# L0 cross-attention: the keys' reciprocal norms spread to their head's rows by transfers, and the scores at another place of the step

## What is computed

```python
def rmsnorm(x, gamma, eps=1e-08):
    n = jnp.linalg.norm(x, axis=-1, keepdims=True) * x.shape[-1] ** (-0.5)
    return x / jnp.maximum(n, eps) * gamma
xn = layernorm(x, ln_x_g, ln_x_b)
ln = layernorm(latents, ln_l_g, ln_l_b)
q = (ln @ Wq)...                      # 16 heads of 64
kv = jnp.concatenate([xn @ Wkv, ln @ Wkv], axis=1)
qn = rmsnorm(q, qn_g) * scale
kn = rmsnorm(k, kn_g)
sim = jnp.einsum('bhid,bhjd->bhij', qn, kn)
sim = jnp.where(padded_mask[:, None, None, :], sim, max_neg)
attn = jax.nn.softmax(sim.astype(jnp.float32), axis=-1).astype(sim.dtype)
out = jnp.einsum('bhij,bhjd->bhid', attn, v)
return out.transpose(0, 2, 1, 3).reshape(b, m, h * d) @ Wout + bout
```

## Time and profile before

| | |
|---|---|
| median of 3 runs | 3399.54 us (3392.83 to 3403.0) |
| the profiled execution | 3395.09 us, its span 3392.6 us |
| TensorE busy | 2876.9 us (85%) |
| VectorE, ScalarE, GpSimd busy | 1615.2, 1080.2, 508.4 us |
| granted TensorE clock, mean | 0.92 |
| DMA | 215.22 MB, 63 GB/s over the span |
| key steps of the L0 cross-attention | 91.0 to about 1310 us, 64 steps |

### The profile page before, as it was taken

How to read it: one execution, slowest core, us unless ns; L and a number is a source line. 1 busy time by engine, 2 the same in 40 slices (tenths; PEclk the granted TensorE clock), 3 DMA queues, 4 the chain that set the end, 5 groups by cost and what they waited for, 6 DMA issues and landing times. The chain is left out here.

```text
span 3392.6 us, 44228 instructions
## 1 busy us (share of the span) xinstructions
PE 2876.9 (85%) x17908; PEld 1943.1 (57%) x17908; DVE 1615.2 (48%) x3651; ACT 1080.2 (32%) x1931; POOL 508.4 (15%) x280
## 2 busy tenths in 40 slices
PE   4899999999999998579999968998964769588756
PEld 2465656666665665445565634665952449577644
DVE  4445454545545443425555545773531340355454
ACT  2233333333333331213555536641321423111121
POOL 2011020202011000000000002770010140244200
PEclk8899999999999999689999989998977879899877
DMA  3000000000000000030101000114857149423101
GB/s 132 0 1 22 1 22 22 1 22 1 22 1 22 1 1 4 27 134 21 40 20 40 1 6 23 45 35 176 312 192 252 55 149 311 166 87 108 31 1 31
DMA packets 80798, 215.22 MB, mean 63 GB/s; under 512 B 5328, under 2 KB 53992, under 8 KB 73944
## 3 DMA queue, kind: packets, MB, share of 16 engines
q1 hardware_dynamic: 77624, 204.32, 18.0%
q0 software_dynamic: 2976, 8.13, 0.7%
HBM read 201.33 MB, written 10.58 MB: 62 GB/s over the span
## 5 line engine op out<-in xcount | busy, mean ns | idle before, releaser
L1328 PE MATMUL L_xattn_bank<-L_xattn_keys_tok,L_xattn_probsT 119*128 119x257 f32 (+1 forms) x1792 | 437.6, 389 | 1.4 <-ACT L_xattn_probsT L1161 1.4
L1262 PE MATMUL L_xattn_wide<-L_xattn_keys_feat,weights_a 128*128 128x512 f32 (+2 forms) x1024 | 388.3, 524 | 3.0 <-DVE L_xattn_max L997 1.3
L1328 PEld LDWEIGHTS L_xattn_bank<-L_xattn_keys_tok,L_xattn_probsT 119*128 119x128 f32 (+1 forms) x1792 | 324.3, 189 | 112.3 <-ACT L_xattn_probsT L1161 42.6
L1155 ACT ACTIVATE L_xattn_scores<-L_xattn_scores,L_xattn_neg_max 128x833 f32<-128x833 f32 x128 | 119.7, 983 | 627.8 <-DVE L_xattn_neg_max L1002 627.8
L1262 PEld LDWEIGHTS L_xattn_wide<-L_xattn_keys_feat,weights_a 128*128 128x128 f32 x1024 | 190.6, 192 | 157.9 <-issue 128.8
L2267 DVE TENSOR_TENSOR_SCAN L_attn_state<-L_attn_decay,L_attn_banks 128x1024 f32<-128x1024 f32 x80 | 182.7, 2286 | 69.5 <-PE L_attn_banks L2469 61.5
L987 DVE TENSOR_TENSOR L_xattn_k_normed<-L_xattn_wide,L_xattn_k_normed 128x834 f32<-128x834 f32 x128 | 125.5, 1022 | 172.8 <-PE L_xattn_wide L1276 172.8
L1544 DVE CUSTOM_DVE_ANT_0 L_xattn_scores<-L_xattn_banks,L_xattn_mask 128x512 f32<-128x512 f32 (+1 forms) x256 | 131.5, 570 | 151.8 <-issue 151.8
L1082 POOL TENSOR_TENSOR L_xattn_keys_tok<-L_xattn_keys_tok,weights_a 119x1792 f32<-119x1792 f32 (+2 forms) x24 | 61.1, 2545 | 939.2 <-DVE L_xattn_keys_tok L922 939.2
L2373 POOL TENSOR_TENSOR L_attn_state<-L_attn_state,L_attn_C_rows 128x1024 f32<-128x1024 f32 x80 | 188.7, 2360 | 70.2 <-DVE L_attn_state L2267 70.1
L2469 PEld LDWEIGHTS L_attn_banks<-L_attn_B_diagonal,L_attn_dt_u_tok 128*128 128x128 f32 x1280 | 150.2, 193 | 66.3 <-issue 64.7
(11 more groups left out here) (498 smaller groups left out, 4691.2 us busy)
## 6 DMA issues: line engine op xcount, KB each, us to landing
L_xattn_ctx_feat<-in_ctx_feat SPq DMA_DIRECT2D x24, 1601.0 KB, 10.3
L_ffn_expert_w<-in_x_L_ffn SPq DMA_DIRECT2D x16, 2056.0 KB, 8.6
L_ffn_expert_w<-in_x_L_ffn SPq DMA_DIRECT2D x15, 1028.0 KB, 7.6
L_ffn_expert_w<-in_x_L_ffn SPq DMA_DIRECT2D x15, 1024.0 KB, 8.4
L_xattn_keys_tok<-in_ctx_tok SPq DMA_DIRECT2D x8, 1547.0 KB
L_attn_C_rows<-L_attn_c_rows SPq DMA_DIRECT2D x48, 256.0 KB, 3.3
L_xattn_ctx_tok<-in_ctx_tok SPq DMA_DIRECT2D x8, 1536.0 KB
L_xattn_ctx_tok_and_one<-in_ctx_tok SPq DMA_DIRECT2D x8, 1536.0 KB
```

What stands on the lines that cost most here:

```text
L1262: last = nc.tensor.matmul(wide[:, 2 * h + c, 0:n], wk[:, k, p * P:(p + 1) * P], xnT[b % 2][:, k, a:a + n], start=(k == 0), stop=(k == KT - 1))
L1328: last = nc.tensor.matmul(bS[:, 0:D + 1], pT[0:r, c, a, :, :].rearrange("p h q -> p (h q)"), xn[b % 2][0:r, t, :], start=(t == 0), stop=(t ...
```

## The change

The four products of `spread` go. In their place ScalarE, behind the second activation of `key_rnorm`, issues eight DMAs: for each quarter j and head h one, whose source is the single SBUF row `rk[32 j + h]` of 417 numbers and whose destination is the 64 rows of that head in a new SBUF tile `spread[:, j, :]`. `keys_normed` waits for all eight (8 x 16 on `k_scale_moved`), and multiplies two SBUF operands.

Since the four banks are then free once `key_clamp(s + 1)` has read bank 0, `scores(s)` waits for that clamp and for the keys of its own step, not for those of s + 1. `swap_max`, `shift` and `exponentials` of step s move into iteration s, behind the scores; `keys_normed(s + 1)` moves behind `shift(s)` on VectorE, ahead of the context work and of `divide`. TensorE's list becomes: keys half 0, turn_weights 0 and 1, keys half 1, turn_weights 2 and 3, turn_mixed, 4 tiles of mix, means, 2 tiles, scores, apply_v, 5 tiles, swap_max, 3 tiles. The tiles of mix are taken in another order, so that the first need ScalarE's copies alone.

```diff
@@ @@
+    MIX_ORDER = [(c, a) for part in (range(4), range(4, HALF_T)) for c in range(2) for a in part]
...
+        spread = sb("k_scale", [P, 4, QK])
...
                 def keys_normed(s):
-                    dve.wait_ge(k_spread, s + 1)
+                    dve.wait_ge(k_scale_moved, 128 * (s + 1))
                     for x in range(2):
                         k = kn[:, s % 2, 2 * x * QK:2 * (x + 1) * QK].rearrange("p (a n) -> p a n", n=QK)
-                        nc.vector.tensor_tensor(k, wide[:, 2 * x:2 * x + 2, 0:QK], k, ALU.mult).then_inc(kn_ready, 1)
+                        nc.vector.tensor_tensor(k, spread[:, 2 * x:2 * x + 2, :], k, ALU.mult).then_inc(kn_ready, 1)
...
                     nc.scalar.activation(rk[:, :], rk[:, :], ACT.Exp, scale=-0.5).then_inc(k_rnorm, 1)
+                    act.wait_ge(k_rnorm, 2 * s + 2)
+                    if s >= 1:
+                        act.wait_ge(kn_ready, 2 * s)
+                    for j in range(4):
+                        for h in range(2):
+                            row = rk[32 * j + h:32 * j + h + 1, :].unsqueeze(1)
+                            nc.scalar.dma_start(spread[h * DH:(h + 1) * DH, j, :], row.broadcast_to([1, DH, QK])
+                                                ).then_inc(k_scale_moved, 16)
...
                 def scores(s):
                     b, p = divmod(s, NQ)
-                    pe.wait_ge(kn_ready, 2 * min(s + 1, STEPS - 1) + 2)
-                    if s + 1 == STEPS:
+                    pe.wait_ge(kn_ready, 2 * s + 2)
+                    if s + 1 < STEPS:
+                        pe.wait_ge(k_clamped, s + 2)
+                    else:
                         pe.wait_ge(s_taken, 2 * s)
...
@@ VectorE's iteration @@
-                    if behind:
-                        shift(s - 1)
...
                     if s < STEPS:
                         score_max(s)
+                    if s >= 2:
+                        keep_result(s - 2)
+                    if s < STEPS:
+                        shift(s)
+                    if turns:
+                        keys_turned(b + 1, p - 5, 1)
+                    if ahead:
+                        keys_normed(s + 1)
...
@@ ScalarE's iteration @@
                     if behind:
-                        exponentials(s - 1)
+                        weights_turned(s - 1, 0)
...
                     if turns:
                         keys_turned(b + 1, p - 5, 0)
                         keys_turned(b + 1, p - 5, 1)
+                    if s < STEPS:
+                        exponentials(s)
...
@@ TensorE's iteration @@
                     if behind:
-                        swap_max(s - 1)
+                        turn_weights(s - 1, 0)
+                        turn_weights(s - 1, 1)
                     if ahead:
                         keys(s + 1, 1)
                     if behind:
-                        turn_weights(s - 1, 0)
-                        turn_weights(s - 1, 1)
+                        turn_weights(s - 1, 2)
+                        turn_weights(s - 1, 3)
                     if s >= 2:
                         turn_mixed(s - 2)
                     if behind:
-                        turn_weights(s - 1, 2)
-                        turn_weights(s - 1, 3)
+                        mix(s - 1, range(4))
                     if ahead:
                         means(s + 1)
-                    if behind:
-                        mix(s - 1, range(5))
-                    if ahead:
-                        spread(s + 1)
-                    if s >= 2:
-                        apply_v(s - 2)
                     if turns:
                         turn_keys(b + 1, p - 5, 0)
                         turn_keys(b + 1, p - 5, 1)
                     if behind:
-                        mix(s - 1, range(5, 10))
+                        mix(s - 1, range(4, 6))
                     if s < STEPS:
                         scores(s)
+                    if s >= 2:
+                        apply_v(s - 2)
...
                     if behind:
-                        mix(s - 1, range(10, TILES))
+                        mix(s - 1, range(6, 11))
+                    if s < STEPS:
+                        swap_max(s)
+                    if behind:
+                        mix(s - 1, range(11, TILES))
```

More of the change, by code:

```diff
@@ L1035, in _ @@
                     turns = b + 1 < B and p in (5, 6)
-                    if behind:
-                        shift(s - 1)
                     if ahead:
                         key_copy(s + 1, 0)
+                    if behind:
+                        weights_turned(s - 1, 1)
+                    if ahead:
                         key_copy(s + 1, 1)
                     if behind:
-                        weights_turned(s - 1, 1)
                         weights_turned(s - 1, 3)
@@ L1053, in _ @@
                         score_max(s)
-                        if turns:
-                            keys_turned(b + 1, p - 5, 1)
-                        if b + 1 < B:
-                            if p == 1:
-                                ctx_stats(b + 1, 0)
-                            if p == 2:
-                                ctx_stats(b + 1, 1)
-                                ctx_norm(b + 1, 0)
-                            if p == 3:
-                                ctx_norm(b + 1, 1)
+                    if s >= 2:
[4 more added lines that the diff above has]
+                        keys_turned(b + 1, p - 5, 1)
+                    if ahead:
+                        keys_normed(s + 1)
+                    if s < STEPS and b + 1 < B:
+                        if p == 1:
+                            ctx_stats(b + 1, 0)
+                        if p == 2:
+                            ctx_stats(b + 1, 1)
+                            ctx_norm(b + 1, 0)
+                        if p == 3:
+                            ctx_norm(b + 1, 1)
                     if behind:
@@ L1185, in _ @@
                     if behind:
-                        weights_turned(s - 1, 0)
+                        weights_turned(s - 1, 2)
                     if ahead:
                         key_square(s + 1, 1)
-                    if behind:
-                        weights_turned(s - 1, 2)
                     if s >= 2:
@@ L1255, in keys @@
                         pe.wait_ge(xT_dve, 4 * b + 4)
-                    if s == 1:
-                        pe.wait_ge(kn_ready, h + 1)
-                    elif s:
+                    if s == 1 and h == 0:
+                        pe.wait_ge(k_clamped, 1)
+                    if s >= 2:
                         pe.wait_ge(s_taken, 2 * (s - 2) + h + 1)
@@ L1271, in means @@
                     last.then_inc(k_meaned, 1)
-                def spread(s):
-                    pe.wait_ge(k_rnorm, 2 * s + 2)
-                    for j in range(4):
-                        last = nc.tensor.matmul(wide[:, j, 0:QK], L.const[32 * j:32 * (j + 1), C_SPREAD:C_SPREAD + P],
-                                                rk[32 * j:32 * (j + 1), :], start=True, stop=True)
-                    last.then_inc(k_spread, 1)
                 def scores(s):
                     b, p = divmod(s, NQ)
-                    pe.wait_ge(kn_ready, 2 * min(s + 1, STEPS - 1) + 2)
-                    if s + 1 == STEPS:
+                    pe.wait_ge(kn_ready, 2 * s + 2)
+                    if s + 1 < STEPS:
+                        pe.wait_ge(k_clamped, s + 2)
+                    else:
                         pe.wait_ge(s_taken, 2 * s)
@@ L1321, in mix @@
                         pe.wait_ge(pT_even, 2 * s + 2)
-                        pe.wait_ge(pT_odd, 2 * s + 2)
                         if s >= 1:
                             pe.wait_ge(oh_ready, s)
-                    for t in tiles:
+                    if tiles[0] == 4:
+                        pe.wait_ge(pT_odd, 2 * s + 2)
+                    for i in tiles:
+                        c, a = MIX_ORDER[i]
+                        t = c * HALF_T + a
                         r = key_rows(t)
-                        c, a = divmod(t, HALF_T)
                         last = nc.tensor.matmul(bS[:, 0:D + 1], pT[0:r, c, a, :, :].rearrange("p h q -> p (h q)"),
-                                                xn[b % 2][0:r, t, :], start=(t == 0), stop=(t == TILES - 1))
+                                                xn[b % 2][0:r, t, :], start=(i == 0), stop=(i == TILES - 1))
                     if tiles[-1] == TILES - 1:
@@ L1355, in _ @@
                 means(0)
-                spread(0)
                 for s in range(STEPS + 2):
```

5 lines of the change are left out of this document (2 added, 3 removed).

## The result

| | median us | runs | ratio to before (95% interval) |
|---|---|---|---|
| before | 3396.18 (3389.75 to 3403.0) | 4 | |
| after | 5028.25 (5025.39 to 5029.6) | 4 | 1.4804 (1.4771 to 1.4837) |

A forecast was written before the change was run, and what follows sets the result against it. TensorE, 85% busy, bounds the kernel; the transfers then set the loop: 43.1 + 2.9 = 46.0 a step, 63 of them 2898, plus context 79, less 1199: +1778; 3399.5 + 1778 + 15 = about 5190 us, range 3385 to 5450.

The forecast's parts named there:

- the case that I chose: L0 cross-attention's eight transfers a step go one after the other at one row group's rate; 4700 to 5450 us, chance 0.50.
- The order of the step: TensorE's rearranged step in the L0 cross-attention: 17.2 us, about 1.1 less than before, if nothing new waits.
- The loop: From means to the next means through VectorE's multiplication: 2.85 + D + 6.95 = 9.8 + D us.
- D: First issue to last landing of a step's eight transfers: 33.3 us, 854 KB at one eight-row group's 26.6 GB/s plus 1.2.
- The threshold of 7.4: The step stays at 17.2 us only while D is under 7.4 us.
- In sequence: Transfers of one queue go in order, taken from two mask transfers ahead of L1 that stood at 205 GB/s; chance 0.50.
- Rival 1: The two groups of source rows are read side by side: D 17.3, 4170 us; chance 0.20, partly so included.
- The clock, +2.9 a step: TensorE idles over 20 us a step, so its part in the loop runs at the lower clock: +2.9, step 46.0 us.
- Context work in the loop: VectorE's context work stands behind the multiplication, so in the loop: 11.2 us a batch, 79 for 7 batches.
- The signs: Multiplication's wait is VectorE's longest, over 20 us a step; landing near 30 us; DMA near full at 27 GB/s; clock 0.5 to 0.7.
- Rival 2: A one-row source is as fast as any: D 5.4, transfers hidden behind the maxima, 3388 us; chance 0.22.
- Rival 3: A row alone is slower than its group: 10 GB/s, D 85, step 98, 8400 us; chance 0.05.

The follow-up runs named there:

- e2: After without its eight transfers; the multiplication reads a tile of ones: 3295.0 us, ratio 0.9712 to before.
- e1: After with each transfer's source 64 different rows instead of one, same issues, bytes and destinations: 3486.5 us, ratio 1.0259 to before.
- e11: After with the norms stored to HBM and broadcast from there by SP, context work ahead of keys_normed: 3410.0 us, ratio 1.005 to before.
- e4: After with quarters 2 and 3 (rows 64, 65, 96, 97) issued by SP, the others by ScalarE: 4271 us.
- e10: After with two issuing queues split by head, so both read the same row group: 4962 us.
- e3: After with the quarters in the order 0, 2, 1, 3, still from one queue: 4694 us.
- e13: After with each of the eight transfers reading a row of another group, still one queue: 4095 us.
- e5: After with all eight transfers issued by SP, ScalarE free: 5060 us.
- e9: After with VectorE's context work moved ahead of keys_normed: 4960 us.

## Why the prediction was right, and where its terms were off

5028 lies 3% under the 5190 forecast, also inside the narrower range of the case that I chose (4700 to 5450), and the stage is slow by the path that I named: one group's rate, in the loop through the multiplication.

- **The order of the step**, 17.2 forecast, 17.24 in e2. Its gain of 1.1 a step is real, and never reached in after.
- **The loop, 9.8 + D.** A row of each kernel: e1 7.74 gives 17.42, e11 8.25 gives 17.92, so 9.67 beside D at the full clock. (The terms that I listed behind the landing add up to 6.79, not 6.95; 6.90 is measured.) After 32.57 gives 43.16 and e4 20.35 (a turning step, 1879.75 to 1900.10 us) gives 31.25: 10.6 and 10.9. The difference from 9.7 is the clock. The threshold of 7.4 held: e11 stands 0.85 over it and loses 0.7 a step.
- **D, 33.3 forecast, 32.57 measured** (32.4 on average). The group's rate was the right pick between 5.4 and 85: 25 to 27 GB/s at an engine share near 0.9, and e4 against e10 shows that the group and not the row or the queue sets it. The Trainium skill (page "SBUF — State Buffer", section "Door 1: The DMA port swizzle") puts rows 0, 1, 32 and 33 on one port and 64, 65, 96 and 97 on another; e4, e10, e3 and e13 agree with that map. That a group has eight rows no run here shows.
- **In sequence** was right for this order of the rows, not as a rule, and so in part by luck: the mask stretch, from which I took it, has two transfers. e3 and e13 overlap from one queue. Rival 1, the two groups side by side, needs two queues or an alternating order; its 4170 for D = 17.3 stands beside e4's 4271 with D = 20.35.
- **The clock, +2.9 a step, was the term mis-sized.** I had the whole chain from landing to issue at the low clock. Where it is, in e5 and in the last batch of after, it takes 12.1 us, 2.3 over 9.8. In the turning steps and the one behind them ScalarE's hold, which I had written adds nothing, brings late work and with it the clock. e9 has no context work in the loop and gives the average: 11.1 us, so 1.3. The clock's 1.6 and D's 0.8 make 2.4 a step (46.0 against e9's 43.57), 63 x 2.4 = 153 us.
- **Context work in the loop**, 79 forecast for seven batches; e9 got 68 back. With the 153 that is the 2977 - 2813.5 = 163 us by which the stage, and the whole (5190 - 5028 = 162), came out shorter.
- **The signs.** VectorE's longest wait is the named one, 1483.5 us or 23 a step. A landing near 30 us was wrong: the issues themselves wait for the queue, so each transfer lands 14.5 us behind its own issue, and 32 us stand for the eight together.
- **Rival 2, hidden,** was out because D was not under 7.4. e1 shows that its 3388 was too low even so: I had 3.2 us of stall in a turning step, and it is 5.9 on average (83/14), as the eight issues take 5.02 and the clock dips behind the stall; and I had 5 us a batch for the context steps, where e1 stands 14 over e2. **Rival 3**, a slower row, is refuted by the rate.

Left open: whether the store through HBM could be given a step's lead, which would need a second buffer of norms and another order of the keys; it wasn't tried.

## What to carry to other kernels

Before a DMA takes the place of an engine's broadcast, count the SBUF rows on its narrow side, source as well as destination: the bytes are those written, but the rate is that of the rows read, here 26 of 425 GB/s. Then write the loop through the new wait as a sum and set the transfer against the threshold it gives; a transfer that is late by 25 us costs each step that, whatever else the change gains. If a narrow source can't be avoided, spread it over row groups, or pass it through HBM, and ask what the issues hold up on the engine that makes them.

## What the runs showed of the hardware

- A VectorE multiplication with both inputs in SBUF took up to 3.99 us instead of 1.02 while GpSimd multiplied in SBUF (e11: 5.49 us for two, which end 0.9 us after GpSimd's 3.83 us instruction does). Before, one input came from PSUM. The Trainium skill has the rule (page "SBUF — State Buffer", section "Who interferes with whom"): such an instruction shares a read port with a GpSimd instruction that reads SBUF, and the port is held for a whole instruction. The trace agrees for GpSimd's multiplications and additions, whose own time grows too (3.17 to 3.83 us). It does not in e2: there a multiplication of two SBUF inputs ran beside the last 0.9 us of GpSimd's mask instruction (8-bit input, from SBUF) in 1.02 us, in all seven batches.
- One queue overlaps neighbouring transfers that read different row groups: from first issue to last landing 32.3, 26.3 and 17.3 us with one, three and seven changes of group among the same eight transfers.
- An engine held by its DMA issues can save time, where its late work keeps TensorE's clock up: with ScalarE held 22.4 us a turning step takes 41.7 to 42.5 us, with ScalarE free 42.6 to 44.4; without turning work both settle at 44.4.
- A broadcast of one 6.7 KB row from HBM to 64 rows landed in 5.0 us (417 KB, two side by side), while one of 104 KB from an SBUF row took 4.07 us in a steady stream.
